# Prefix attention's programs placed behind the experts' in the same block, and a mask product over the local keys alone

## The reference

```
h = layernorm(x) * (1 + ca) + sa;  x = x + ga * attention0(h)     # linear attention, 16 heads of 8
h = layernorm(x) * (1 + cb) + sb;  x = x + gb * experts(h)        # 16 experts of 64, 4 chosen per token, one shared
h = layernorm(x) * (1 + ca) + sa;  x = x + ga * attention1(h)     # prefix attention, 16 heads of 8
h = layernorm(x) * (1 + cb) + sb;  x = x + gb * transformer(h)    # two layers of local attention and feed-forward
```

## Time and profile before

| | us |
|---|---|
| median of 3 runs (lowest, highest) | 1427.15 (1425.95, 1428.6) |
| profiled execution | 1425.69 |
| its span | 1423.9 |
| PE, DVE, ACT, POOL busy | 1278.2, 1064.5, 869.0, 740.8 |

### The profile page before, as it was taken

One profiled execution on the slowest core, in us unless ns is written; L12 is line 12 of the kernel. 1 busy time (PEld: TensorE's weight loads), 2 busy tenths in 40 slices (PEclk: granted clock), 3 DMA queues, 4 the chain that ended last, 5 costly groups with the idle time before them and its releaser, 6 DMA issues.

```text
span 1423.9 us, 39853 instructions
## 1 busy us (share of the span) xinstructions
PE 1278.2 (90%) x16225; PEld 992.1 (70%) x16225; DVE 1064.5 (75%) x2355; ACT 869.0 (61%) x2064; POOL 740.8 (52%) x595
## 2 busy tenths in 40 slices
PE   6878899979999999983899999987879999998887
PEld 6767778847777777762688888864557888887554
DVE  6956865348788888874899898855679989898465
ACT  5632222236666666652799989853449999997521
POOL 7345554423343434333877777733247777777010
PEclk9899999959999999995999999999999999999999
DMA  4052354000000000003000101001100000000011
GB/s 147 30 121 54 69 119 103 18 13 3 3 3 3 3 4 3 4 3 97 8 10 9 24 9 33 2 9 31 25 25 12 9 18 16 10 5 9 13 38 47
DMA packets 62038, 41.49 MB, mean 29 GB/s; under 512 B 41233, under 2 KB 51873, under 8 KB 61729
## 3 DMA queue, kind: packets, MB, share of 16 engines
q1 hardware_dynamic: 61280, 38.68, 11.2%
q10 hardware_dynamic: 576, 0.27, 0.1%
HBM read 28.17 MB, written 2.37 MB: 21 GB/s over the span
## 4 chain that ended last, share of the span: by engine, by line
PE 35%; SPq 7%; DVE 5%; POOL 2%; ACT 2%; issue 2%; DMA 1%; DVEq 0%; POOLq 0%; ACTq 0%
SPq L1769 5%; PE PS L2296 4%; PE PS L2282 4%; PE PS L2273 4%; PE PS L2246 4%; PE PS L2316 4%; PE PS L2214 3%; PE PS L2216 3%; PE PS L2215 3%; PE PS L2307 2%; PE PS L2261 2%; PE PS L2385 1%; PE PS L2376 1%; POOL rn L1836 1%; DVE qk L1943 1%
## 5 line engine op out<-in xcount | busy, mean ns | idle before, releaser
L1843 POOL TENSOR_TENSOR rot<-qk,sinl 128x1024 f32<-128x1024 f32 x64 | 218.1, 3408 | 107.7 <-DVE qk L1943 107.7
L1836 POOL TENSOR_TENSOR rn<-ss,neghalf 128x16 f32<-128x16 f32 x64 | 210.3, 3286 | 39.8 <-DVE ss L1936 39.1
L2122 ACT ACTIVATE e_pm<-PS,e_mx 128x128 f32<-128x128 f32 x512 | 151.6, 372 | 18.7 <-DVE e_mx L1927 18.7
L1402 DVE TENSOR_REDUCE d_mx<-PS 128x4 f32<-128x576 f32 x128 | 96.9, 757 | 66.1 <-PE PS L1546 63.2
L422 POOL TENSOR_TENSOR m_work<-m_work,cb 128x512 f32<-128x512 f32 x64 | 83.1, 1300 | 87.3 <-DVE m_work L1066 87.3
L814 ACT ACTIVATE m_work<-PS 128x512 f32<-128x512 f32 x72 | 43.0, 597 | 136.8 <-PE PS L604 136.8
L1465 ACT ACTIVATE pa<-PS 128x512 f32<-128x512 f32 x128 | 76.4, 597 | 61.6 <-PE PS L1555 61.5
L2214 PE MATMUL PS<-wqkv_hi,e_h_hi 128*128 128x512 f32 x192 | 91.3, 475 | 19.5 <-DVE e_h_lo L1920 19.5
L1066 DVE TENSOR_TENSOR m_work<-m_work,PS 128x512 f32<-128x512 f32 x72 | 49.6, 688 | 77.2 <-ACT m_work L814 76.4
L1546 PEld LDWEIGHTS PS<-kx,d_q 32*64 32x64 f32 x2048 | 66.4, 133 | 48.6 <-issue 32.8
L2081 ACT ACTIVATE qk<-PS 128x512 f32<-128x512 f32 x128 | 76.9, 603 | 36.4 <-PE PS L2216 36.3
(11 more groups left out here) (272 smaller groups left out, 3613.0 us busy)
## 6 DMA issues: line engine op xcount, KB each, us to landing
cb<-comb_rows SPq DMA_DIRECT2D x32, 512.0 KB, 9.4
zs<-Z SPq DMA_DIRECT2D x64, 32.0 KB
zg<-Z SPq DMA_DIRECT2D x16, 128.0 KB
out_x<-X SPq DMA_DIRECT2D x8, 256.0 KB, 2.6
zs<-Z SPq DMA_DIRECT2D x64, 31.8 KB
zg<-Z SPq DMA_DIRECT2D x16, 127.0 KB
X<-in_L_attn_x SPq DMA_DIRECT2D x3, 512.0 KB, 8.1
wqkv<-in_e_wqkv SPq DMA_DIRECT2D x2, 768.0 KB, 4.4
```

What stands on the lines that cost most here:

```text
L1402: chain(dve.tensor_reduce(mx[:, par, :, :], s, AX.X, ALU.max))
L1836: pool.tensor_tensor(rn[:, v % 2, :], ss[:, v % 2, :], c.neghalf[:, :], ALU.pow).then_inc(rn_ready.sem, 1)
L1843: pool.tensor_tensor(rot[:, :, :, :], x, bc(sinl[:, t, :, :], 2, H2), ALU.mult).then_inc(rot_ready.sem, 1)
L2122: last = act.activation(pm[:, v % 2, h, r, j, :], PS[:, SBANK + r, at * KEYS2:(at + 1) * KEYS2], ACT.Exp, bias=mx[:, v % 2, r, at:at + 1])
```

## The change

- `windowed_attention` no longer opens blocks. It returns its five programs, each cut into a first part without dependence (`fill`, `zero`), an `early(s)` that is called in each experts' step, and a `main`. `front` calls them in its own programs: `main` follows the experts' loop on each engine, PE's behind a wait for the last add.
- `early` spreads the two prologues over the steps: the prefix keys and values of sequence b over the six steps from START[b] = 50, 54, 58 and 66 on, one tile each and in a bank of its own, and the fronts of units 0 and 1 over steps 63 to 71.
- `routed(s)` is true for steps with k = 11 to 19 of a round. There DVE does `weigh(s)` itself, directly behind `product(s)`, and PE waits for a semaphore of its own. POOL's `gate_down` moves to steps 13, 14 and 15 of 18.
- In the front, weights that are needed late are loaded late, layer 0's modulation is worked out in two parts (columns of shift and scale first, the other four behind `queries(0)`), `gate_rows` follows `queries(1)`, `bias_rows` is DVE's and works on 3 x one row in place of 128, and some statistics move behind others' work in DVE's order.
- From the second tile on (t > 0) the mask's product writes only the 2 x 128 columns of local keys; the prefix keys' product is then the first to write its columns after the bank was opened.
- To make room, the front's temporaries lie in tiles that prefix attention or Z own later.

The core of the diff (line numbers of the changed kernel differ from those of the profile):

```diff
-                sp.dma_start(wmod[0], A["L0_wmod"]).then_inc(mod_loaded[0].sem, 16)
+                sp.dma_start(wmod[0][:, 0:2 * D], A["L0_wmod"][:, 0:2 * D]).then_inc(mod_loaded[0].sem, 16)
...
                 for s in range(NS):
                     weigh(s)
-                    if s // (2 * NU) + 1 < B and s % (2 * NU) in (3, 4, 5):
-                        ex.gate_down(pool, c, s // (2 * NU) + 1, s % (2 * NU) - 3)
+                    if s // (2 * NU) + 1 < B and s % (2 * NU) in (13, 14, 15):
+                        ex.gate_down(pool, c, s // (2 * NU) + 1, s % (2 * NU) - 13)
...
+                    early(s)
+                main()
...
+                    early(s)
+                pe.wait_ge(gated.sem, gated.at(NS))
+                pe.wait_ge(added.sem, added.at(NG8))
+                main()
...
+                def weigh(s):
+                    g, k = divmod(s, NU)
+                    ready = comb_loaded[g % 2][k // (1 + NJ // 2)]
+                    dve.wait_ge(ready.sem, ready.at(32 * (g // 2 + 1)))
+                    dve.wait_ge(gated.sem, gated.at(s + 1))
+                    dve.tensor_tensor(uu[:, s % 4, :], uu[:, s % 4, :], cb[g % 2][:, ORDER[k], :], ALU.mult)\
+                       .then_inc(u_ready_d.sem, 1)
...
                 for s in range(NS):
                     product(s)
+                    if routed(s) and s % NU:
+                        weigh(s)
...
                 stats(0)
+                bias_rows()
+                mods(0, range(0, 2), 1)
                 stats(1)
-                mods(0)
-                gates(0)
                 stats(2)
-                stats(3)
-                stats(4)
-                stats(5)
                 maxima(0)
                 shift(0)
+                mods(0, range(2, 6), 2)
+                gates(0)
                 sums(0)
                 invert(0)
+                stats(3)
...
+        def early(s):
+            if s in (67, 69):
+                front_t((s - 67) // 2)
+            if s in (68, 70):
+                front_qkv((s - 68) // 2)
+            if at(s, 2) is not None:
+                first_t(at(s, 2))
+            if at(s, 3) is not None:
+                first_k(at(s, 3))
+            if at(s, 5) is not None:
+                first_v(at(s, 5))
...
+            hidden = 2 * W1 if t else KEYS1
+            for i in range(2):
+                pe.matmul(out[:, i, :, 0:hidden], identb[:, :], bc(mask[:, min(t, 1), 0:hidden], 1, 2),
+                          start=True, stop=True)
```

More of the change, by code:

```diff
@@ L10 @@
+from collections import namedtuple
 from contextlib import ExitStack
@@ L219, in gate_down, with front @@
                            ALU.mult).then_inc(self.w_gated.sem, 1)
-def front(c, A, ex):
+def front(c, A, ex, then):
     nc, X, PS, ident, identb, signal = c.nc, c.X, c.PS, c.ident, c.identb, c.counter
@@ L305, in slot, with routed, by_pool, by_dve @@
             return NC + 2 * r + st
+        def routed(s):
+            return any(lead(s, k) for k in range(11, 20))
+        def by_pool(s):
+            return sum(1 for i in range(s + 1) if i % NU and not routed(i))
+        def by_dve(s):
+            return sum(1 for i in range(s + 1) if i % NU and routed(i))
         def lead(s, k):
@@ L466, in _, with mods @@
             def _(pe):
-                def mods(l):
-                    pe.wait_ge(mod_loaded[l].sem, 16)
-                    for k in range(6):
+                def mods(l, which):
+                    pe.wait_ge(mod_loaded[2 if l == 0 and which[0] else l].sem, 16)
+                    for k in which:
                         last = pe.matmul(PS[:, LB, M0 + (6 * l + k) * B:M0 + (6 * l + k + 1) * B], wmod[l][:, k * D:(k + 1) * D],
@@ L633, in _ @@
                 queries(0)
+                mods(0, range(2, 6))
                 values(1)
@@ L642, in _ @@
                 turn_q(0)
+                mods(1, range(0, 6))
                 context(1)
@@ L692, in _ @@
                 attend(7)
+                early, main = then.tensor(pe)
                 for s in range(NS + 2):
@@ L1072, in add @@
                                       ALU.add).then_inc(added.sem, 1)
+                dve.memset(bq[0:96, :], 0.0).then_inc(cond_ready.sem, 1)
+                fill, early, main = then.vector(dve, steps, added)
+                fill()
                 dve.memset(c.neghalf[:, :], -0.5)
@@ new lines, in ssb @@
+    def ssb(name, shape, dt=F32):
+        return c.sb(name, shape, dt, sc)
+    wqkv = ssb("d_wqkv", [P, 3 * D])
+    wo = ssb("d_wo", [P, D])
+    hmask = ssb("hmask", [P, 4])
+    pmask = ssb("pmask", [P, 8])
+    mask32 = ssb("mask32", [P, 2, KEYS1])
+    mask = ssb("mask", [P, 2, KEYS1], BF16)
+    kx = ssb("kx", [P, B, 4, 3 * W1 + PRE])
+    kraw = ssb("kraw", [P, 2, P])
+    q = ssb("d_q", [P, B, P])
+    vv = ssb("vv", [P, B, H1, 2, VW1])
+    vpre = ssb("vpre", [P, B, 2, 8, VW1])
+    hrep = ssb("hrep", [P, B, 8, PRE])
@@ new lines, in first, with unit, spot, at @@
+    def first(b):
+        return b + 1 if b < 3 else 6
+    def unit(v):
+        return v + 4 if v < 2 else v + 5
+    def spot(b):
+        return b % 2, 1 + b // 2
+    def at(s, k):
+        return START.index(s - k) if s - k in START else None
+    def tile(u):
+        return u // B, u % B
+    def xt(u):
+        return X[:, TB * (u % B) + u // B, :]
+    def sync(sp):
+        for dst, src in ((wqkv[:, :], A["d_wqkvT"]), (wo[:, :], A["d_woutT"]), (hmask[:, :], A["c_hmask"]),
+                         (pmask[:, :], A["c_pmask"]), (mask32[:, :, :], A["c_mask1"])):
+            sp.dma_start(dst, src).then_inc(w_loaded.sem, 16)
```

979 lines of the change are left out of this document (485 added, 494 removed).

## The result

The changed kernel takes 1406.31 us (median of 4 runs, 1402.88 to 1415.42) against 1427.88 of the kernel before beside it. The ratio is 0.9869, 95% interval 0.9834 to 0.9904. The profiled execution took 1406.71 us (span 1404.9), 18.98 less than the one of before (1425.69). The forecast was 1394.2 with a range that ended at 1404.0: the direction was right, but the gain between the profiled executions was forecast as 33.0 us and is 19.0 (the medians lie 21.6 apart).

What follows compares the result with a forecast made beforehand. Bounds: PE, busy throughout the last experts but waiting on DVE earlier, and short chains at the half-clock handoff. -24.0 + 5.2 - 12.0 - 2.2 + 0 = -33.0 us; against the 1427.15 median, 1394.2 us, range 1386.5 to 1404.

Steps and rivals of the forecast that it cites:

- (e): Front, 0 to 81 us: waits won and work added on DVE balance, 0 us, ends -4.6 and +2.8.
- rival (2): Front keeps its lead because PE and ACT, not DVE's work, set its pace: -4.6 us, about 1389.6; chance 0.14.
- (a): Handoff from last add to unit 1's scores: 10.6 us in place of 34.6, -24.0 us, ends -24.3 and -20.4.
- rival (1): Clock falls at the handoff, unit 0 at half clock: 3.6 us more, about 1397.8; chance 0.14.
- (b): Prologues inside the experts' steps 50 to 71: added PE matmuls cost +5.2 us, work on other engines covered.
- rival (4): Inserted steps tie in-order queues together, ACT waiting for a late transpose: slower, about 1430 us; chance 0.03.
- (c): Experts' steps with k = 11 to 19: multiply moved from POOL to DVE, -12 us, ends 0 and -13.
- (d): Prefix attention from the second tile: mask's product on 256 columns instead of 288, -2.2 us, ends 0 and -3.0.
- three quarters: Narrower mask: share of its 3.0 us assumed kept despite PE's wait for the exponential, giving -2.2 us.
- The rest: After prefix attention, where the change reaches nothing: 0 us.
- (3): Experts: multiply on DVE takes 1.30 us and eats the gain, three rounds give nothing, 1406 us; chance 0.09.
- (5): Narrower mask changes nothing, the weight load behind it sets the pace: +2.2, 1396.4 us; within the forecast's 0.60.

Runs made afterwards that it cites:

- fifth experiment: Changed kernel with statistics, second modulation part, gate rows and second modulation back in the old front order; new loads, split and DVE bias rows kept: 1400.4 us, ratio 0.982.
- fourth experiment: Changed kernel with three added TensorE products that nobody reads, in front of its waits at the handoff: 1400.6 us, ratio 0.983 to the kernel before.
- experiment 1: Changed kernel with the statistics of tiles 3 to 5 back in front of the first maximum on DVE: 1404.6 us, ratio 0.987 to the kernel before.
- experiment 2: Changed kernel with TensorE's second modulation product moved to right behind the gate rows: 1408.6 us, ratio 0.988 to the kernel before.
- eighth experiment: Changed kernel with every multiply on POOL and POOL's w2g products back at steps 3 to 5: 1414.9 us, ratio 0.991 to the kernel before.
- ninth experiment: Changed kernel with the mask's product over all 288 columns for every tile: 1411.3 us, ratio 0.989 to the kernel before.
- eleventh: Changed kernel with POOL's w2g products back at steps 3 to 5, the moved multiplies left on DVE: 1408.4 us, ratio 0.987 to the kernel before.
- third experiment: Changed kernel with transposes and features of the fourth batch's prefix counted fifth and unit 1's sixth, as they are made: 1400.9 us, ratio 0.984 to the kernel before.
- experiment 10: Changed kernel with only one added TensorE product, in front of the wait for the last add: 1403.3 us, ratio 0.984 to the kernel before.

## Why the prediction was wrong

**(e) The front, 0 forecast, +5.5 measured.** This is the step that failed. The forecast put the first maximum at 15.4; it came at 17.45. The second tile's normalisation, which PE's order puts in front of the first queries, ended on ACT at 14.28 and not at 13.5, and the transposes and queries behind it took 2.9 us, not 1.8. The estimate then took DVE as the engine that sets the pace, on the ground that it had hardly a gap from 20 to 76 us in the kernel before, and reckoned only with what the change adds to DVE. But DVE had no gap because of the old order: the statistics and the gates stood in front of the first maximum, and the second modulation in front of the context product. Moved behind them, they are links in chains through PE, POOL and ACT. DVE was busy 6.78 of 10 us from 30 to 40, against 9.51 before and 9.31 in the fifth experiment. So a lead of 2.6 us, in place of 4.6, was followed by a stretch to the first product that is 8.0 us longer (76.54 against 68.50), in place of 4.6. The fifth experiment shows that the order did it: the same work in the old order has a lead of 2.0 at the first maximum and keeps 1.7 of it up to the experts. The forecast had this as rival (2) at -4.6 and gave no case to a front that gets slower by its order; its upper end was +2.8.

**(a) The handoff, -24.0 forecast, -22.0 measured.** The mechanism was right: the first scores 0.11 us behind the add, and at whole clock unit 1 9.96 us behind it (fourth experiment). What came on top was rival (1). Its price of 3.6 us was for a whole unit at half clock; it was 2.8 here (13.90 - 11.11). At whole clock the fill was 0.6 shorter than the forecast said (9.96, not 10.6), which hid a part of it. The chance of 0.14 for rival (1) was far too small: all 10 profiles with early prologues and fewer than three covers have half clock behind the handoff. In five of them (experiments 1, 2, 8, 9, 11) it went on for 24 to 27 us, and the two pieces from the add to unit 31 together took 325.8 to 327.4 us, against 316.5 with the covers. The Trainium skill, "TensorE: Matmul & The Clock Gate", section "What's actually happening", lets half rate return only after an idle window. By that rule alone gaps under a microsecond cost nothing; the row of 290 to 295 us at 0.50, among gaps of 0.81, 0.83, 0.96 and 0.79, does not bear that out.

**(b) The prologues inside the experts, +5.2 forecast, +5.9 measured.** That the sum came out close is luck. The matmuls, priced at 5.2, cost 3.7 at most, and 2.2 came from two stalls that were put at nothing: 1.6 from a wait for one count too many (third experiment), 0.6 from a w2g product and a multiply of POOL beside the first prologue's normalisation (eighth and eleventh). For the first, the text had the mechanism in rival (4) and found it worth nothing below 0.9 us of slack; it did not ask which count each wait names.

**(c) The multiply, -12.0 forecast, -10.6 measured** (eighth experiment: 10.9, or 10.3 with the 0.6 that it gives back behind step 50). Its length was right (0.69), the waits fell to 4.0 as forecast (below 6). In round 2 the eight steps from 19 to 27 took 22.4 us in place of 25.9, so 3.4 were won where 4.0 stood, and the other rounds missed by as much. The term was mis-sized by a tenth: a multiply starts 0.79 us behind the product and so adds that much to DVE's step, not 0.72, and 24 of them make 1.7 us. No run separates this from the rest of the estimate.

**(d) The mask, -2.2 forecast, -1.6 measured** (ninth experiment: 0.055 a unit over 28 units). A pair went from 0.34 to 0.31 or 0.32, and the wait for the exponential took back 0.03 a unit, as the text said; three quarters was too much.

**The rest, 0 forecast, +3.7 measured.** The sum was made against one profiled execution and leaned on its clock where nothing was changed. The second profile of the changed kernel has 796.9 there, 4.1 less. A forecast for one execution needs a width for that; this one had none. The second four runs have a median of 1403.3, which lies inside the range; so how far the whole time is from the forecast depends on the runs by 3 us. The loss in the front does not: it is in every profile with that order.

Of the rivals, (1) happened, (2) and (3) did not, (4) happened at steps 68 and 69 at 1.6 us, (5) did not. The six misses, 5.5 + 3.7 + 2.0 + 0.7 + 1.4 + 0.6, all had one sign and make 13.9 of the 14.0 us.

## What to carry to other kernels

Read an engine without gaps as "it has work in front of it", not as "it sets the pace": when a change moves work of that engine behind a dependent chain, follow the chain through every in-order queue. To test it, undo the moves together as well as one by one: here one alone gave 0.8 or 1.2 us, and uncovered another wait or made one, while all of them gave 7. Where work moves into another loop, write down for every counting semaphore the order in which its signals are made in that loop; if two kinds of step swap places, their counts must swap too. At a handoff whose gaps are short but several, price the slower clock as the likely case, and cover the gaps with matmuls that nobody reads: three of 0.8 to 0.9 us gave back 2.8 here, and by the pieces of the profiles where the half clock lasted (325.8 to 326.7 from the add to unit 31, against 316.5) they would have been worth 9 to 10 there, an estimate. Where a move takes work off an engine, look at what the rest of its queue now runs beside.

## What was not expected of the hardware

- Idle stretches of 0.8 to 1.0 us brought half clock in all ten profiles without three covers, 3.0 to 5.7 us behind the add. Not all of the gaps were needed: in experiments 1 and 3 the clock fell at 3.0 and 3.4 us, before the last gap, which then did not come, and filling the one before the scores changed nothing (13.94 against 13.90 us). In both profiles with three covers, where only the 0.81 us before the last down products were left, it did not fall.
- How long it then stayed differed between executions: 7 us (the changed kernel twice, experiments 5 and 10), 10 (experiment 3), 24 (experiments 2, 8, 9 and 11) or 27 (experiment 1), though PE had no gap in most of that time. Three rows of experiment 1:

```profile
295.00:300.00 5.00, 5.00 (x81) 3.75 (x84) 2.00 (x5) 2.04 (x8) 0.17 (x1) 0.50 0.00 0
300.00:305.00 5.00, 5.00 (x87) 3.27 (x79) 2.18 (x6) 2.39 (x6) 0.86 (x1) 0.50 0.02 3
305.00:310.00 5.00, 5.00 (x66) 3.44 (x69) 1.61 (x4) 1.82 (x5) 0.73 (x2) 0.50 0.00 0
```

- What decides between them was not found; no run here was made for it. Between profiled executions the long stay costs some 7 us more than the short one (326 against 319.3 from the add to unit 31). How much of the spread of single runs it makes (1401.6 to 1413.4 us for one and the same kernel in experiment 1) is not shown, for only one run of each has a trace.
- A small DVE instruction beside POOL's work can take eight times its length: 1.34 and 1.32 us for two of the gates in experiment 1, which take 0.17 alone.
